# Second node phase of a four-layer graph network: the inverse counts arrive already spread over all partitions, the leaky step becomes one VectorE operation, ScalarE makes the moments, GpSimd the product of mean and root

## The reference, cut to what matters

```python
def _gcn_layer(x, src, dst, ew, Ws, bs, Wn, bn, bias):
    n = x.shape[0]
    msg = x[src] * ew[:, None]
    agg = jax.ops.segment_sum(msg, dst, num_segments=n)
    agg = agg + x
    cnt = jax.ops.segment_sum(jnp.ones_like(ew), dst, num_segments=n) + 1.0
    neigh = agg / cnt[:, None]
    out = x @ Ws.T + bs + neigh @ Wn.T + bn + bias
    return jnp.where(out > 0, out, NEG_SLOPE * out)
...
for l in range(N_LAYERS):
    x = _gcn_layer(x, src, dst, social_edge_weights, W_self[l], b_self[l], ...)
return x @ W_agg.T + b_agg
...
x = _layernorm(x + _L0_gnn_ref(x, edge_index, edge_weight, ...), axis=-1)
```

## Time and profile before

| | us |
|---|---|
| median of three runs | 4166.23 |
| profiled execution | 4162.3 |
| its span, first to last instruction | 4160.5 |
| TensorE busy in the span | 3536.3 |
| VectorE busy | 3183.2 |
| GpSimd busy | 2943.0 |
| ScalarE busy | 2582.3 |

### The profile page before, as it was taken

One profiled execution on the slowest core, in us unless ns is written; L12 is line 12 of the kernel. 1 busy time (PEld: TensorE's weight loads), 2 busy tenths in 40 slices (PEclk: granted clock), 3 DMA queues, 4 the chain that ended last, 5 costly groups with the idle time before them and its releaser, 6 DMA issues.

```text
span 4160.5 us, 79758 instructions
## 1 busy us (share of the span) xinstructions
PE 3536.3 (85%) x18468; PEld 2206.8 (53%) x18576; DVE 3183.2 (77%) x11794; ACT 2582.3 (62%) x5498; POOL 2943.0 (71%) x3125
## 2 busy tenths in 40 slices
PE   5674999999678999687899999996688775789997
PEld 2211444588433566333799999996234442234454
DVE  7654755466865788854688888887997999987998
ACT  5593257633136788644587778786156774267888
POOL 3765554477776899777566666664775998775888
PEclk8795999999899999899999999998899998999999
DMA  3334467788346788555555555552477885577887
GB/s 82 84 97 76 136 203 233 263 281 281 120 132 233 253 285 288 167 155 178 173 182 180 180 179 180 182 183 84 121 217 237 263 263 166 151 233 261 289 288 233
DMA packets 532695, 810.51 MB, mean 195 GB/s; under 512 B 126084, under 2 KB 180550, under 8 KB 532254
## 3 DMA queue, kind: packets, MB, share of 16 engines
q1 hardware_dynamic: 392991, 545.93, 42.3%
q10 hardware_dynamic: 85166, 154.99, 10.0%
q0 software_dynamic: 54096, 104.47, 9.5%
HBM read 493.19 MB, written 311.11 MB: 193 GB/s over the span
## 4 chain that ended last, share of the span: by engine, by line
PE 51%; DVE 19%; POOL 14%; issue 8%; DMA 3%; DVEq 2%; ACT 2%; POOLq 1%; ACTq 0%; SPq 0%
PE ps L1661 14%; DVE hit L1122 4%; PE ps L1825 4%; POOL records_by_dst L695 4%; POOL got L746 4%; PE ps L1806 4%; PE ps L1807 4%; POOL rstd L781 3%; PE ps L1728 2%; PE ps L1727 2%; PE ps L1785 2%; PE ps L1786 2%; PE ps L1816 2%; PE ps L1694 2%; PE ps L1743 2%
## 5 line engine op out<-in xcount | busy, mean ns | idle before, releaser
L1661 PE MATMUL ps<-hit,rest 128*128 128x512 bf16 x2296 | 714.5, 392 | 94.7 <-DVE hit L1122 89.5
L781 POOL TENSOR_TENSOR rstd<-vare,neg_half 128x4 f32<-128x4 f32 x490 | 557.6, 1138 | 218.0 <-DVE vare L1187 182.1
L1661 PE MATMUL ps<-hit,got 128*128 128x512 bf16 x1148 | 451.1, 393 | 221.2 <-DVE hit L1122 84.4
L1388 ACT ACTIVATE evac<-ps 128x512 f32<-128x512 f32 x392 | 234.2, 597 | 642.8 <-PE ps L1661 634.0
L746 POOL DMA_INDIRECT got<-nodes_l,sorted_by_dst x392 | 400.0, 1020 | 132.6 <-issue 112.5
L1661 PEld LDWEIGHTS ps<-hit,got 128*128 x1172 | 117.0, 100 | 562.2 <-issue 466.1
L1215 DVE TENSOR_TENSOR nT<-sums,ps 128x512 f32<-128x512 f32 x392 | 263.0, 671 | 171.1 <-PE ps L1706 137.1
L1373 ACT ACTIVATE ps<-zeros 128x512 f32<-128x512 f32 x588 | 344.3, 598 | 59.3 <-DVEq L443 34.1
L1661 PEld LDWEIGHTS ps<-hit,rest 128*128 x2344 | 234.9, 100 | 241.3 <-issue 36.1
L746 POOL DMA_INDIRECT got_pair<-in_x,sorted_by_dst x196 | 197.3, 1007 | 201.9 <-PE ps L1661 130.8
L1410 ACT ACTIVATE aff<-ps,shift,rstd 128x128 f32<-128x128 f32 x784 | 290.8, 447 | 1.3 <-POOL shift L797 1.2
(11 more groups left out here) (298 smaller groups left out, 10101.0 us busy)
## 6 DMA issues: line engine op xcount, KB each, us to landing
nodes_l<-xout SPq DMA_DIRECT2D x196, 256.0 KB, 3.2
xin<-nodes_l SPq DMA_DIRECT2D x196, 256.0 KB, 3.7
sums<-sums_l SPq DMA_DIRECT2D x196, 256.0 KB, 2.9
sums_l0a<-evac_pair ACTq DMA_DIRECT2D x98, 256.0 KB
sums_l<-evac_pair ACTq DMA_DIRECT2D x98, 256.0 KB
sums<-sums_l0a SPq DMA_DIRECT2D x98, 256.0 KB
sums_l0b<-evac ACTq DMA_DIRECT2D x98, 256.0 KB
sums<-sums_l0b SPq DMA_DIRECT2D x98, 256.0 KB
```

Of the source, the lines that this page charges most:

```text
L781: pool.tensor_tensor(rstd[:, n, at, :], vare[:, n, at, :], neg_half[:, :], ALU.pow)\
L1388: act.activation(w.evac[h][:, slot, :], ps[:, BANKS * h + g % BANKS, :], ACT.Copy).then_inc(s["out"].sem, 1)
L1661: last = pe.matmul(into, part.rearrange("p a d -> p (a d)"), w.hit[:, w.place(i), :], start=False, stop=False, skip_group_check=True)
```

## The change

The inverse counts of the first layer are written a second time to DRAM, as one f32 row per group (`inverse_l0_row`), and `d1` loads them into `inv_all`, spread over all partitions by the transfer, as `d2` does. The spread product goes away, and the mean on VectorE multiplies two SBUF operands. ScalarE makes only `below`, now 0.2 times the biased product, with no positive part; VectorE adds the bias to the PSUM product and takes the larger of the two in one operation, which gives `x2T`; the join on GpSimd goes away. ScalarE makes the negated mean and the variance after VectorE's aggregates. GpSimd multiplies mean and root right behind the root, and VectorE keeps only the lift. The buffer `xres` moves behind `inv_all`.

```diff
@@ -111,6 +111,7 @@
+        inv_d["l0_row"] = dram("inverse_l0_row", (GROUPS, ROWS))
@@ -222,6 +223,7 @@
+        inverse_l0 = front("inverse_l0", [GROUPS, ROWS])
@@ -295,9 +297,11 @@
-        xres = node("xres", [P, 4, K, D])
...
+        behind = node.at
+        xres = node("xres", [P, 4, K, D])
+        node.at = behind
@@ -403,7 +407,7 @@
-                    "d1": "root0 tx xT add iv nT mm act x2 y res var rstd norm",
+                    "d1": "root0 tx xT add nT mm act x2 y res aggr var scaled rstd norm",
@@ -561,10 +565,11 @@
+            sp.dma_start(inv_d["l0_row"], inverse_l0[:, :]).then_inc(s_partst, 16)
...
-            sp.wait_ge(s_partst, 48)
+            sp.wait_ge(s_partst, 64)
@@ -645,7 +650,7 @@
-            nodes("d1", [("rows", xin, x1_d), ("sums", sums, sum_d["l0b"]), ("inv", inv3, inv_d["l0"])], ["tx", "nT"],
+            nodes("d1", [("rows", xin, x1_d), ("sums", sums, sum_d["l0b"]), ("all", inv_all, inv_d["l0_row"])], ["tx", "nT"],
@@ -753,14 +758,6 @@
-            def join(i, q, slot):
-                s = node_s["d1"]
-                held(*s["act"](i + 1))
-                if later(i, 2):
-                    held(*s["y"](i - 1))
-                pool.tensor_tensor(x2T[:, slot % 2, :], above[:, slot % 2, :], below[:, slot % 2, :], ALU.subtract)\
-                    .then_inc(s["x2"].sem, 1)
-
@@ -771,7 +768,7 @@
-            def power(phase, n, ready, done, shifted=True):
+            def power(phase, n, ready, done):
@@ -780,8 +777,6 @@
-                    if not shifted:
-                        return
@@ -837,7 +832,7 @@
-            beside("d1", ("add", "x2", "root0"), lambda: pipeline(pool, GROUPS, 8, [(add_x, 4), (join, 8), (power("d1", 0, "var", None, False), 12)]))
+            beside("d1", ("add", "scaled"), lambda: pipeline(pool, GROUPS, 8, [(add_x, 4), (power("d1", 0, "var", "scaled"), 12)]))
@@ -972,6 +967,8 @@
+                if name == "l0":
+                    dve.tensor_copy(inverse_l0[:, :], inverse[:, :])
@@ -1076,7 +1073,7 @@
-            dve.tensor_scalar(b_below[:, :], b_l0b[:, :], -SLOPE, None, ALU.mult)
+            dve.tensor_scalar(b_below[:, :], b_l0b[:, :], SLOPE, None, ALU.mult)
@@ -1242,17 +1239,34 @@
-                def shifts(i, q, slot):
-                    dve.wait_ge(*s["root0"](i + 1))
-                    at = slot % 4
-                    dve.tensor_tensor(shift[:, 0, at, :], negmean[:, 0, at, :], rstd[:, 0, at, :], ALU.mult)
+                def mean(i, q, slot):
+                    dve.wait_ge(*s["add"](i + 1))
+                    if later(i, 4):
+                        dve.wait_ge(*s["mm"](i - 3))
+                    dve.tensor_tensor(nT[:, slot % 4, :], sums[:, slot, :], inv_all[:, slot, :], ALU.mult).then_inc(s["nT"].sem, 1)
+
+                def leaky(i, q, slot):
+                    dve.wait_ge(*s["act"](i + 1))
+                    if later(i, 2):
+                        dve.wait_ge(*s["y"](i - 1))
+                    dve.scalar_tensor_tensor(out=x2T[:, slot % 2, :], in0=ps[:, 4 + slot % 2, :], scalar=b_l0b[:, 0:1],
+                                             in1=below[:, slot % 2, :], op0=ALU.add, op1=ALU.max).then_inc(s["x2"].sem, 1)
+
+                def rows(i, q, slot):
+                    for k in range(K):
+                        dve.bn_stats(stat[:, 0, k, :], res[:, slot % 4, k, :])
+
+                def halves(i, q, slot):
+                    for k in range(K):
+                        last = dve.bn_aggr(mv[:, 0, slot % 4, k, :], stat[:, 0, k, :])
+                    last.then_inc(s["aggr"].sem, 1)
...
+                    dve.wait_ge(*s["scaled"](i + 1))
...
-                stats = row_stats((10, 0, res, s["var"]))
-                pipeline(dve, GROUPS, 8, [(average(s, 0, "add"), 5), (residual, 10), (shifts, 13), SETTLE, (lift, 13)] + stats[1:])
+                pipeline(dve, GROUPS, 8, [(leaky, 8), (mean, 5), (residual, 10), (lift, 13), SETTLE, (rows, 10), SETTLE, (halves, 10)])
@@ -1448,11 +1462,11 @@
-                    act.activation(above[:, slot % 2, :], ps[:, 4 + slot % 2, :], ACT.Relu, bias=b_l0b[:, :])
-                    act.activation(below[:, slot % 2, :], ps[:, 4 + slot % 2, :], ACT.Relu, bias=b_below[:, :], scale=-SLOPE)\
+                    act.activation(below[:, slot % 2, :], ps[:, 4 + slot % 2, :], ACT.Identity, bias=b_below[:, :], scale=SLOPE)\
...
-                pipeline(act, GROUPS, 8, [(leaky, 7), (copy_xT(s), 3), (norm("d1", xout, "norm", None), 13)])
+                pipeline(act, GROUPS, 8, [(leaky, 7), (copy_xT(s), 3), (moments("d1", slice(0, 1), "var"), 11),
+                                          (norm("d1", xout, "norm", None), 13)])
@@ -1735,10 +1749,12 @@
+                    if first(i):
+                        groups_out(pe, "d1", GROUPS)
...
-                        pe.wait_ge(*s["act"](i - 1))
+                        pe.wait_ge(*s["x2"](i - 1))
@@ -1754,7 +1770,7 @@
-                pipeline(pe, GROUPS, 8, [(final, 9), (products, 6), (transposes(s, "d1", 3), 2), (spread(s, 0, 3, "d1"), 4)])
+                pipeline(pe, GROUPS, 8, [(final, 9), (products, 6), (transposes(s, "d1", 3), 2)])
...
```

## The result

The changed kernel takes 4206.86 us (median of four runs, 4203.90 to 4212.63), the kernel before 4165.81 in the same job: a ratio of 1.0103, 95% interval 1.0089 to 1.0118. It is 41 us slower, where 26 us faster was forecast. The time lies 1.9 us above the top of the range and beside the 4206 that rival A gave for a late start.

A forecast was written before the change was run, and what follows sets the result against it. TensorE was taken to bound the second node phase at 3.69 us per group; a period of 3.40 saves 28 us, plus 2 for the head and 0.5 for the front: -26, 4166.2 to 4140 us, range 4130 to 4205.

The forecast's parts named there:

- rival A: Second node phase: VectorE's lift waits out GpSimd's sum every group, period 4.45 us, 0.76 a group lost; chance 0.18.
- late start: Second node phase: the lift's collision with GpSimd's sum begins only at the 35th group, +37 us, 4206 with the head.
- the comparison of VectorE's lap with TensorE's period: Second node phase, per group: VectorE's sum 3.30, at most 3.36 us, stays below TensorE's 3.37.
- the period of 3.40: Second node phase: each of 98 groups takes 3.40 instead of 3.69 us, saving 28 us.
- TensorE's new wait for the leaky rows: TensorE's self-weight product waits for VectorE's rows of two groups before; costs nothing while VectorE keeps its lead.
- ScalarE and GpSimd: Second node phase, per group: ScalarE needs 2.9 to 3.1 us, GpSimd 2.7 and becomes the idlest.
- DMA: Second node phase: five transfers a group take 3.47 us; prefetch just covers a deficit of 0.10 us per group.
- Rival B: Second node phase: DMA engines bound it, five transfers take 4.0 us a group, +33 us, 4199; chance 0.11.
- rival C: Second node phase: gain eaten up by DMA at 350 to 364 GB/s or passing collisions, 4160 to 4174; chance 0.15.
- Head and front: Fuller queues at the phase's head cost 2 us, the 196 KB row at the front's end 0.5 us.

The follow-up runs named there:

- e5: Changed kernel with row statistics of the first 104 of 128 columns: 4127.96 us, ratio 0.9916.
- e2: Changed kernel with ScalarE copying 256 columns of the transposed rows a second time in every group: 4138.13 us, ratio 0.9938.
- e12: Changed kernel with ScalarE's two moments moved ahead of its copy of the transposed rows, no work added: 4135.64 us, ratio 0.9934.
- e10: e1 with a sixth transfer of 256 KB in every group, in the same queue: 4176.06 us, ratio 1.0030.
- e1: Changed kernel with the lift (128x4, plus 1.0) moved from VectorE to ScalarE: 4123.68 us, ratio 0.9902.
- e4: Changed kernel with row statistics of the first 64 of 128 columns: 4126.87 us, ratio 0.9911.
- e6: Changed kernel with row statistics of 104 of 128 columns and one added VectorE delay in group 20: 4195.75 us, ratio 1.0077.
- e7: Changed kernel with row statistics of 64 of 128 columns and one added VectorE delay in group 20: 4127.54 us, ratio 0.9917.
- e3: Changed kernel with ScalarE's copy of the transposed rows moved ahead of below: 4169.69 us, ratio 1.0016.

## Why the prediction was wrong, point by point

The step that failed is the comparison of VectorE's lap with TensorE's period: "Sum 3.30, at most 3.36. That lies below TensorE's 3.37, but with next to no margin", and with it the period of 3.40. VectorE measured 3.33, inside its bounds. TensorE was the mis-sized term: 3.26 instead of 3.37. The spread product took more with it than its own 0.32, by TensorE's starts in order of time, first of the kernel before, then of the changed one:

```profile
1508.36 0.60 PE L1694 MATMUL ps<-ident,xin 128*128 128x128 f32 x4
1508.89 0.39 PE L1706 MATMUL ps<-inv,ones_bf 3*128 3x512 bf16 x1
```

```profile
1388.55 0.60 PE L1708 MATMUL ps<-ident,xin 128*128 128x128 f32 x4
1388.99 0.38 PE L1725 MATMUL ps<-bias,ones_bf 128*128 128x512 bf16 x1
```

The four transposes take 0.53 us to the start of a spread product and 0.44 to that of a bias product, which itself goes from 0.23 to 0.21. (The chain of the earlier trace rows goes by modelled ends and shows the same 0.11 behind the spread product: 0.32 from 1505.59 to 1505.91 for the bias product.) I had read how long the product lasts, and not how long the others last without it. VectorE, whose measured lap was 0.04 ahead of TensorE's period by my sum, was 0.07 behind it, which is the very point from which I had said that rival A decides; e5 shows that 0.10 us less on VectorE turns the result into a gain of 36 us. It shows too that the 0.04 of my sum would have been next to nothing: with 0.03 the lift is caught before the phase is over.

- *TensorE's new wait for the leaky rows*: free while VectorE led, as forecast, and 0.8 us a group (50.8 / 63) after it had lost its lead.
- *ScalarE and GpSimd*: in the first groups both had time to spare (26 and 24 us busy of 30), as forecast. That ScalarE gets shorter stands in the forecast as a relief and in rival A as the shorter loop; e2 and e12, which make that way longer again, show that rival A had it right.
- *DMA*: sized too high, 3.47 with prefetch to cover a deficit; it is 3.25 (e10). Rival B and the lower speeds of rival C are out. The Trainium skill (HBM Reference, Specifications (TRN2)) has what I did not weigh: one core that streams alone goes well above its share of 358 GB/s, to some 425. This case's trace gives 403 at the limit.
- *Head and front*, 2.5 us: no run shows them. e1 saves 39.2 us where 98 x (3.69 - 3.26) = 42 are due, but its first normalisation starts at 1386.7, as in the other two kernels, and its last at 1695.9: between them 38.4 of 97 x 0.43 = 41.7 are saved. What is missing lies behind the head.
- *Rival A*: right in mechanism and place, and in its signs (lift near 1.2 us, period near 4.4, ScalarE waiting for the shift). Its price was 0.76 a group and is 0.61: I counted 3.18 from the start of the lift and then added the whole hold of 1.27 which contains the lift. It began at the 11th lift, not the 35th group, because VectorE lost 0.07 us a group and then 0.43 at once. That its late start came to 4206 is luck: 63 groups at 0.76 were forecast and 77 at 0.61 came, 48 and 47 us. The range was to reach over that start and stops 1 us short of it. Its chance of 0.18 was too low for a state that needs one slip to enter, holds itself, and stood 0.9 us away: slips of 1.08 and 0.99 us were in the earlier trace rows.

What the 0.43 us of idle time at 1417 is, the trace names only as issue; it stays open. It is no accident of one run: a pause of 0.42 or 0.43 us stands ahead of the same aggregates, between the tenth lift and the eleventh, in e2, e4, e5, e6, e7 and e12 too (1412.89 to 1418.18). At 0.07 a group the remaining 0.33 would have gone in five more groups without it.

## What to carry to other kernels

When two engines block each other, compare more than their busy times: follow the way from the end of the blocked operation round to the next start of the blocking one, and set it against what the blocked engine needs from that same end to its next request (3.00 against 3.16 here). If the way is the shorter by less than the blocking operation lasts, the collision repeats in every round, and a round lasts as long as the way and the blocking operation together. So speeding up an engine on that way can close a loop that was open; in a loop that is closed it still pays (e3). Cheap remedies are to take the small operation to an engine that the blocking one does not hold off, as ScalarE in e1 (0.19 to 0.21 us in every group), or to change the order so that the way gets longer; an operation of 0.16 us can be worth 83. A lead is worth as much as the spare time that restores it: 0.03 us a group did not outlast the pauses of e5.

## What the runs showed of the hardware that was not expected

The blocking is not symmetric in the way that I had read from the earlier trace rows. In e1 GpSimd's root starts 0.05 us ahead of VectorE's mean, and neither is longer than alone; in the first groups of the changed kernel, the second pair of rows, the mean starts 0.10 us ahead, and the root lasts 1.47.

```profile
1600.20 1.02 POOL L778 TENSOR_TENSOR rstd<-vare,neg_half 128x4 f32<-128x4 f32 x1
1600.25 0.69 DVE L1246 TENSOR_TENSOR nT<-sums,inv_all 128x512 f32<-128x512 f32 x1
```

```profile
1384.80 0.69 DVE L1246 TENSOR_TENSOR nT<-sums,inv_all 128x512 f32<-128x512 f32 x1
1384.90 1.47 POOL L778 TENSOR_TENSOR rstd<-vare,neg_half 128x4 f32<-128x4 f32 x1
```

So a root that is under way does not hold up a mean, but a mean that is under way holds up a root. The Trainium skill (SBUF — State Buffer, Who interferes with whom) says that whoever is first keeps the shared pair of ports for its whole instruction; that fits the sum, the join and the mean here, and does not fit the root. A lift that asks 0.03 us ahead of the sum gets through (e12, 4136 us), one that asks 0.06 us (e6, 4196) or 0.16 us (the changed kernel, 4207) behind its start waits out the rest of it, group after group.
